# First attention of a Flamingo-style block: the query bias by full-width products, zero writes moved in the load queue, weight splits dealt out otherwise

## The chip, the cores and the metric

The kernel is one program on one core of a Trainium2 chip. The metric is device time in microseconds (us) of one execution; the time quoted is the median of several executions. Engines are named as in the profile: PE (matrix products), PEld (its weight loads), DVE, ACT, POOL (the vector, activation and general engines) and SP, which here only issues transfers. ACTq and SPq are the issuing sequencers of ACT and SP.

## The reference

Eight batches of 256 rows x 256 columns pass through four residual parts: attention over 120 context rows, a mixture of experts with two of twelve experts per row (eight real, four that return the row itself), a second attention with 16 heads, and a product in 8-bit floats. The change touches the first of them and the work that lies beside it:

```python
x = x + jnp.tanh(g_xattn[0]) * _L0_xattn_ref(_layernorm(x, axis=-1), ctx_512, ctx_512, ...)
x = x + jnp.tanh(g_ffn[0]) * _L0_ffn_ref(_layernorm(x, axis=-1), ...)
...
q = jnp.einsum('bld,de->ble', query, Wq) + bq
k = jnp.einsum('bld,de->ble', key, Wk) + bk
v = jnp.einsum('bld,de->ble', value, Wv) + bv
scores = jnp.einsum('bqe,bke->bqk', q, k)
attn = jax.nn.softmax(scores, axis=-1)
out = jnp.einsum('bqk,bke->bqe', attn, v)
```

The query bias `bq` reaches the scores as one number per key, `bq . k`, the same for every query row.

## The kernel before

The program is written engine by engine, each engine with its own hand-written order; semaphores tie them. The first attention and the gate of the experts run as a software pipeline over `t in range(B + 9)`, B = 8 batches, called slots here. A batch b goes through these functions, each in a later slot of its engine:

- DVE `stats0(b)`, POOL `root0(b)`, ACT `norm0(b)` (L649): the first layer norm. PE `transpose_x0(b)` (L1557), ACT `copy_xT(b)`.
- PE `keys0(b)` (L1531), ACT `copy_kt0(b)` (L623), PE `keys_by_query(b)`: the keys are multiplied by the query weights (L1542) and by the query bias (L1545, a stationary operand of one column, result 1 x 120). DVE `copy_kq(b)` (L991) and `copy_bqk(b)` (L995) bring the two results to SBUF. PE `values0(b)` (L1552), DVE `copy_v0(b)`.
- PE `scores0(b)`: first L1571, which puts the bias row under all 128 query rows of two halves (contraction over one partition, 240 columns), then L1577, the scores proper. DVE `max0_of(b)`, ACT `exp0_of(b)` (L636), PE `transpose_prob(b)` (L1586), ACT `copy_probT(b)` (L643), PE `attend(b)` (L1594).
- DVE `add_x1(b)`, `stats1(b)`, POOL `root1(b)` (L497, L499), ACT `norm1(b)` (L658): the second layer norm. SP stores its result in `xn_d` (L439). PE `transpose_x1(b)` (L1557 again), DVE `copy_xT1(b)` (L1026), PE `gate_of(b)` (L1611), DVE `logits_of(b)` (L1036).

`norm1(b)` writes one of two buffers and so waits for the store of batch b - 2 to have landed:

```python
act.wait_ge(rstd1_ok, b + 1)
...
wait(act, xn_stored[b % 2], 16 * (b // 2))
```

Beside this, the expert weights (8.4 MB) come in as eight loads `chunk_in[0..7]` of four chunks each, and each of the 32 chunks is split into a high part, on ACT by `high(j)` (L668), and a low part, on POOL by `low(j)` (L513) or for four chunks on DVE by `low(j)` (L1032). `low(j)` needs `high(j)`, and both take the chunks in rising order. `HIGH_FROM`, `LOW_FROM`, `LOW_LATE`, `VECTOR_LOW` and `VECTOR_FROM` say from which slot on a place in an engine's slot takes a chunk. Also beside it, `clear_y()` on ACT writes zeros (4.2 MB) into the experts' output buffer `y_d` in HBM by five transfers.

After the slots, DVE picks the two experts of every row (the chain from L1056 `top` over L1059 `eq`, L1060 `cand`, L1064 `pick`, L1065 `hot`, L1068 `left`, first for 12 of the 16 row tiles, `EARLY`, then for the last four), ranks the rows and builds the lists by which POOL gathers rows for the experts. The order on every engine is the order of its loop body; nothing reorders it.

Of the kernel before, what the change touches and what calls it, by code (L numbers as in the profile page):

```python
# [90 lines left out]
def build(nc, x, ctxT, wq0T, wk0, wv0, bq0, bk0, bv0, gateT, gbias, wmoe, wq1, wk1, wv1, wo1,  # L91
          bq1, bk1, bv1, bo1, wfT, bf, gains, c_ident, c_tri, c_count, c_token, c_head, out):
    ctx = ExitStack()
    with ctx:
# [52 lines left out]
        kq = sb("kq", [P, B * C * LK], F32, kv)  # L147
        v0 = sb("v0", [LK, B, D + 1], F32, kv)
        bqk = sb("bqk", [1, B * LK], F32, kv)
# [141 lines left out]
        def sems(names):  # L291
# [11 lines left out]
        (kt_done, kt_ok, kq_done, kq_ok, bqk_ok, v0_done, v0_ok) = sems(  # L303
            "kt_done kt_ok kq_done kq_ok bqk_ok v0_done v0_ok")
# [104 lines left out]
        HIGH_FROM, LOW_FROM = (8, 2, 2, 2), (4, 4, 9, 3)  # L409
        EARLY, FAR = TILES - 2 * U, 64 * P  # L410
        AHEAD, ZERO_LOADS = 6, 1 + 2 * TILES * D // ZEROS
        VECTOR_LOW, VECTOR_FROM = (7, 10, 13, 16), 5
        LOW_LATE = {B: 3, B + 1: 4, B + 2: 3, B + 3: 2, B + 4: CHUNKS}

        @block.sync
        def _(sp):
# [10 lines left out]
            for m in range(LOADS):  # L427
                c = cols(m, PER_LOAD * CHUNK)
                sp.dma_start(wl[:, c].bitcast(F32), wmoe[:, c]).then_inc(chunk_in[m], 16)
                if m == 0:  # L430
                    sp.dma_start(x4[:, 4:B, :], xv[:, 4:B, :]).then_inc(x_late_in, 16)
                    for dst, src in late:
                        sp.dma_start(dst, src).then_inc(con_in, 16)
                    sp.dma_start(bv1_sb[:], bv1.rearrange("o (c p) -> p (o c)", p=P),
                                 allow_slow_non_contiguous=True).then_inc(con_in, 16)
# [172 lines left out]
        def _(act):  # L608
# [69 lines left out]
            def clear_y():  # L678

                act.wait_ge(zero_ok, 1)  # L680
                act.dma_start(xn_d[0:1, :], wh[0:1, E_FFN * WE - D:].bitcast(F32)).then_inc(zeroed, 16)
                y_p = y_d[1:1 + 2 * TILES * P, :].rearrange("(p r) n -> p (r n)", p=P)
                for c in range(0, 2 * TILES * D, ZEROS):
                    act.dma_start(y_p[:, c:c + ZEROS], wh[:, E_FFN * WE - ZEROS:].bitcast(F32)).then_inc(zeroed, 16)

            for t in range(B + 9):
                if t == B - 1:
                    clear_y()
# [8 lines left out]
                high_next(t, 2)  # L697
# [267 lines left out]
        def _(dve):  # L965
# [22 lines left out]
            def copy_kq(b):  # L988

                dve.wait_ge(kq_done, b + 1)  # L990
                dve.tensor_copy(kq[:, cols(b, C * LK)], bank[1][:, 0:C * LK]).then_inc(kq_ok, 1)  # L991

            def copy_bqk(b):
                dve.wait_ge(kq_done, b + 1)
                dve.tensor_copy(bqk[0:1, cols(b, LK)], bank[1][0:1, C * LK:(C + 1) * LK]).then_inc(bqk_ok, 1)  # L995
# [529 lines left out]
        def _(pe):  # L1525
# [9 lines left out]
            def keys_by_query(b):  # L1535
# [3 lines left out]
                wait(pe, bqk_ok, b)  # L1539
# [26 lines left out]
            def scores0(b):  # L1566
                pe.wait_ge(xT_copied, b + 1)
                pe.wait_ge(kq_ok, b + 1)
                pe.wait_ge(bqk_ok, b + 1)
                wait(pe, exp_done, b)  # L1570
                pe.matmul(bank[6][:, 0:U * LK], ones[0:1, :],  # L1571
                          bqk[0:1, cols(b, LK)].unsqueeze(1).to_broadcast([1, U, LK]), start=True, stop=False,
                          skip_group_check=True)
                for u in range(U):
                    for c in range(C):
                        k = b * C * LK + c * LK
                        ins = pe.matmul(bank[6][:, u * LK:(u + 1) * LK], xT[:, b % 2, c * S + u * P:c * S + u * P + P],  # L1577
                                        kq[:, k:k + LK], start=False, stop=(u == U - 1 and c == C - 1),
                                        skip_group_check=True)
# [552 lines left out]
```

## Time and profile before

| | us |
|---|---|
| median of 3 runs | 381.73 (381.43 to 382.63) |
| the profiled execution, its own time | 380.27 |
| its span, first to last instruction | 378.5 |
| slots of the first attention, PE from batch 0's transposes to the last logits | 10.7 to 72.6 |

The rows below are from the profiled execution. A row of a timeline gives start, length, engine, line, operation, tiles, shapes and count; a bracket at the end is the engine's idle time before the row and what ended it. Lengths of neighbouring rows on PE overlap, since products are pipelined; the chain that ended last gives lengths without overlap. Time between the last slot and the end (the experts, the second attention, the last product) is not touched.

### The profile page before, as it was taken

Reading aid. Unit: us, or ns where it says so; the run is one execution under the profiler, and the core shown is the slowest. Engines: PE = TensorE matmul, PEld = TensorE weight load, DVE = VectorE, ACT = ScalarE, POOL = GpSimd, SP = SyncE. Lnnn points to the kernel's source line nnn. Section 1 sums busy time; section 2 is a strip of 40 time slices with the busy share of each in tenths; the row PEclk is TensorE's granted clock in tenths of the full one; section 3 lists DMA queues with packets and bytes.
Section 4 is the critical chain, followed back from the end, with each engine's and each line's share of the span. In section 5 each row is a group of like instructions: output and inputs, shape, how many; then the busy total and the mean of one; then the engine's idle time right before and its main releaser. Section 6 shows DMA issues by size and latency. Waiting matters only on the chain.

```text
span 378.5 us, 9200 instructions
## 1 busy us (share of the span) xinstructions
PE 348.6 (92%) x3030; PEld 277.8 (73%) x3031; DVE 260.1 (69%) x669; ACT 219.1 (58%) x455; POOL 159.2 (42%) x215
## 2 busy tenths in 40 slices
PE   1999999976999999999999998879999999999995
PEld 0888787654799999999999993556667666666773
DVE  1569879895655665555445447878888989776785
ACT  1687899612454445445444542466777778665585
POOL 7497599505355655565555435321131132102000
PEclk9999999999999999999999999999999999999999
DMA  6999752301224334323333214310111000000004
GB/s 184 312 413 399 296 241 85 113 2 55 79 75 134 102 102 132 104 78 69 78 75 76 63 58 138 114 58 5 55 58 57 2 2 2 3 3 2 2 33 189
DMA packets 15386, 38.25 MB, mean 101 GB/s; under 512 B 3574, under 2 KB 4748, under 8 KB 13820
## 3 DMA queue, kind: packets, MB, share of 16 engines
q1 hardware_dynamic: 9978, 22.55, 17.1%
q0 software_dynamic: 3936, 10.45, 9.4%
q10 hardware_dynamic: 1442, 4.85, 3.3%
q8 instruction: 19, 0.31, 0.4%
q14 instruction: 11, 0.09, 0.1%
HBM read 24.34 MB, written 13.50 MB: 100 GB/s over the span
## 4 chain that ended last, share of the span: by engine, by line
PE 77%; DVE 9%; ACT 6%; DMA 3%; issue 3%; POOL 1%; ACTq 1%; DVEq 0%; POOLq 0%
PE two L1716 15%; PE two L1729 14%; PE two L1865 5%; PE two L1748 4%; PE two L1895 4%; PE two L1930 4%; PE two L1851 4%; PE two L1831 3%; PE two L1739 2%; PE two L1577 2%; PE two L1542 2%; PE two L1922 2%; PE two L1557 2%; PE two L1911 1%; DMA kmask<-in_c_head 1%
## 5 line engine op out<-in xcount | busy, mean ns | idle before, releaser
L1207 DVE SCALAR_TENSOR_TENSOR gate<-th,two 128x512 f32<-128x512 f32 x39 | 26.8, 688 | 58.3 <-ACT th L739 32.4
L739 ACT ACTIVATE th<-two 128x512 f32<-128x512 f32 x39 | 23.3, 599 | 70.9 <-PE two L1729 43.1
L546 POOL DMA_INDIRECT y_d<-y_sb,goal_i x39 | 38.4, 986 | 50.7 <-ACT y_sb L749 50.7
L540 POOL DMA_INDIRECT xg<-xn_d,slot_i x39 | 37.8, 970 | 31.2 <-DVE slot_i L1160 13.8
L1716 PE MATMUL two<-wh,gh 128*128 x156 | 44.2, 283 | 0.1
L1716 PE MATMUL two<-wh,gl 128*128 x156 | 44.0, 282 | 0.0
L1716 PE MATMUL two<-wl,gh 128*128 x156 | 43.8, 281 | 0.0
L560 POOL TENSOR_TENSOR rstd<-var,half 128x2 f32<-128x2 f32 x14 | 9.8, 700 | 76.9 <-DVE var L1274 76.9
L1307 DVE TENSOR_REDUCE nm<-two 128x8 f32<-128x960 f32 x32 | 36.1, 1152 | 4.5 <-PE two L1851 4.1
L513 POOL TENSOR_TENSOR wl<-wl,wh 128x512 fp32r<-128x512 f32 x28 | 35.3, 1277 | 7.0 <-ACT wh L668 6.9
L1729 PE MATMUL two<-wh,xh 128*128 x78 | 34.2, 438 | 1.3 <-DVE xl L1201 1.3
L837 ACT ACTIVATE pT<-two 120x1024 f32<-120x1024 f32 x32 | 31.1, 1037 | 7.0 <-PE two L1865 7.0
L1716 PEld LDWEIGHTS two<-wh,gh 128*128 128x128 f32 x156 | 29.5, 189 | 3.6 <-issue 0.3
L1716 PEld LDWEIGHTS two<-wl,gh 128*128 128x128 f32 x156 | 29.4, 188 | 3.3
L1716 PEld LDWEIGHTS two<-wh,gl 128*128 128x128 f32 x156 | 29.4, 188 | 3.2
L1729 PE MATMUL two<-wl,xh 128*128 x78 | 30.9, 396 | 0.0
L1729 PE MATMUL two<-wh,xl 128*128 x78 | 30.7, 394 | 0.0
L1211 DVE TENSOR_TENSOR gl<-two,gh 128x512 fp32r<-128x512 f32 x39 | 27.0, 691 | 2.7 <-ACT gh L744 1.1
L744 ACT ACTIVATE gh<-two 128x512 fp32r<-128x512 f32 x39 | 23.6, 605 | 0.1
L1748 PE MATMUL two<-ident,gate 128*128 128x128 f32 x156 | 23.3, 272 | 0.0
L734 ACT ACTIVATE xh<-two 128x256 fp32r<-128x256 f32 x39 | 15.7, 403 | 9.4 <-PE two L1739 9.4
L971 DVE BATCH_NORM_STATS2 stat<-x_sb 128x6 f32<-128x256 f32 x32 | 12.0, 417 | 11.9 <-DMA x_sb<-in_x 11.7
(272 smaller groups left out, 885.0 us busy)
## 6 DMA issues: line engine op xcount, KB each, us to landing
wl<-in_wmoe SPq DMA_DIRECT2D x8, 1024.0 KB, 14.9
y_d<-wh ACTq DMA_DIRECT2D x4, 1024.0 KB
yg<-y_d SPq DMA_DIRECT2D x7, 512.0 KB, 3.6
xn_d<-xq SPq DMA_DIRECT2D x8, 256.0 KB, 2.0
xz<-xn_d SPq DMA_DIRECT2D x8, 256.0 KB
out_x<-of SPq DMA_DIRECT2D x8, 256.0 KB, 2.0
x_sb<-in_x SPq DMA_DIRECT2D x1, 1024.0 KB, 9.9
x_sb<-in_x SPq DMA_DIRECT2D x1, 768.0 KB, 4.6
```

Of the source, the lines that this page charges most:

```text
L513: pool.tensor_tensor(wl[:, c], wl[:, c].bitcast(F32), wh[:, c], ALU.subtract).then_inc(split_l, 1)
L540: pool.indirect_dma_start(xg[:, n % 2, :], None, xn_d, bass.IndirectOffsetOnAxis(ap=slot_i[:, n:n + 1], axis=0)).then_inc(gathered[n % 2], 16)
L546: pool.indirect_dma_start(y_d, bass.IndirectOffsetOnAxis(ap=goal_i[:, n:n + 1], axis=0), y_sb[:, n % 2, :], None).then_inc(y_stored[n % 2] ...
L739: nc.scalar.activation(th[:], bank[2 + k][:], ACT.Tanh, scale=0.5).then_inc(th_ok, 1)
L744: nc.scalar.activation(gh[:, k, :], bank[4 + k][:], ACT.Copy).then_inc(gh_ok, 1)
L837: nc.scalar.activation(pT[:, r, p, :], ring(ring_of_keys(b, r) + p)[0:LK, :], ACT.Exp).then_inc(e_ok, 1)
L1207: dve.scalar_tensor_tensor(gate[:, k, :], th[:], 1.0, bank[2 + k][:], ALU.add, ALU.mult).then_inc(gate_ok, 1)
L1211: dve.tensor_tensor(gl[:, k, :], bank[4 + k][:], gh[:, k, :], ALU.subtract).then_inc(gl_ok, 1)
L1307: dve.tensor_reduce(nm[:, u, 2 * HG * p:2 * HG * (p + 1)].rearrange("p (j h) -> p j h", j=2), src.rearrange("p j (h k) -> p j h k", k=LK), ...
L1716: ins = pe.matmul(bank[6 + k][:, 0:D], (gl if part == 2 else gh)[:, k, a], (wl if part == 1 else wh)[:, bass.ds(e + (C * FF + c * D), D)], ...
L1729: ins = pe.matmul(bank[2 + k][:], (xl if part == 2 else xh)[:, k, c * P:(c + 1) * P], (wl if part == 1 else wh)[:, bass.ds(e + c * FF, FF) ...
L1748: ins = pe.transpose(bank[4 + k][:, c * P:(c + 1) * P], gate[:, k, c * P:(c + 1) * P], ident[:])
```

## The change

Three edits. The bias product L1545 now has a stationary operand of the whole array (the bias column repeated 128 times), so its result is 128 x 120, is copied with the rest of `kq` in one DVE copy, and feeds L1571's successor from all 128 partitions with a stationary operand that repeats the first column of the identity. `clear_y()` leaves ACT; SP issues the same five transfers ahead of the last two weight loads. The tables that deal out the splits are changed, and ACT skips one place in slots 6 and 7.

```diff
-        kq = sb("kq", [P, B * C * LK], F32, kv)
+        kq = sb("kq", [P, B, (C + 1) * LK], F32, kv)
...
-        HIGH_FROM, LOW_FROM = (8, 2, 2, 2), (4, 4, 9, 3)
+        HIGH_FROM, LOW_FROM = (8, 8, 2, 2), (4, 9, 9, 3)
+        BUSY_SLOTS = (6, 7)
...
-        VECTOR_LOW, VECTOR_FROM = (7, 10, 13, 16), 5
-        LOW_LATE = {B: 3, B + 1: 4, B + 2: 3, B + 3: 2, B + 4: CHUNKS}
+        VECTOR_LOW, VECTOR_FROM = (13, 16, 19, 22), 9
+        LOW_LATE = {B: 3, B + 1: 4, B + 2: 3, B + 3: 3, B + 4: CHUNKS}
...
             for m in range(LOADS):
+                if m == LOADS - 2:
+                    sp.wait_ge(zero_ok, 1)
+                    sp.dma_start(xn_d[0:1, :], wh[0:1, E_FFN * WE - D:].bitcast(F32)).then_inc(zeroed, 16)
+                    y_p = y_d[1:1 + 2 * TILES * P, :].rearrange("(p r) n -> p (r n)", p=P)
+                    for c in range(0, 2 * TILES * D, ZEROS):
+                        sp.dma_start(y_p[:, c:c + ZEROS], wh[:, E_FFN * WE - ZEROS:].bitcast(F32)).then_inc(zeroed, 16)
...
-            def clear_y():
...
-                if t == B - 1:
-                    clear_y()
...
-                high_next(t, 2)
+                if t not in BUSY_SLOTS:
+                    high_next(t, 2)
...
-                dve.tensor_copy(kq[:, cols(b, C * LK)], bank[1][:, 0:C * LK]).then_inc(kq_ok, 1)
-
-            def copy_bqk(b):
-                dve.wait_ge(kq_done, b + 1)
-                dve.tensor_copy(bqk[0:1, cols(b, LK)], bank[1][0:1, C * LK:(C + 1) * LK]).then_inc(bqk_ok, 1)
+                dve.tensor_copy(kq[:, b, :], bank[1][:, 0:(C + 1) * LK]).then_inc(kq_ok, 1)
...
-                    ins = pe.matmul(bank[1][0:1, C * LK:(C + 1) * LK], bq0_sb[:, c:c + 1], kt0[:, b % 2, c, :],
-                                    start=(c == 0), stop=(c == C - 1))
+                    ins = pe.matmul(bank[1][:, C * LK:(C + 1) * LK], bq0_sb[:, c:c + 1].to_broadcast([P, P]),
+                                    kt0[:, b % 2, c, :], start=(c == 0), stop=(c == C - 1))
...
-                pe.matmul(bank[6][:, 0:U * LK], ones[0:1, :],
-                          bqk[0:1, cols(b, LK)].unsqueeze(1).to_broadcast([1, U, LK]), start=True, stop=False,
+                pe.matmul(bank[6][:, 0:U * LK], ident[:, 0:1].to_broadcast([P, P]),
+                          kq[:, b, C * LK:(C + 1) * LK].unsqueeze(1).to_broadcast([P, U, LK]), start=True, stop=False,
```

What the tables do, counted from the code: high parts done by the end of slot 7, 18 before and 10 now (in slots 2 to 7 before three a slot; now two a slot in 2 to 5, one in 6 and 7); before two more stood ahead of `norm1(2)` in slot 8 and now too, so 20 before and 12 now. The rest: before 12 from there to slot 11; now 20, up to slot 13, with four between `norm1(5)` and `norm1(6)` and four between `norm1(6)` and `norm1(7)`, where none stood before. Low parts on POOL before slot 8: 13 before, 9 now. DVE's four stood in slots 5 to 8 and stand in slots 9 to 12.

Three places in the orders. First SP's queue. Before, the last loads are followed by the weights of the last product (`wf_sb`) and the eight stores of the second norm:

```order
L434 DMA bv_sb<-in_bv 128x2x1
L429 DMA wl<-in_wmoe 128x2048 x7
L436 DMA wf_sb<-in_wfT 128x512
L439 DMA xn_d<-xq 128x512 x8
L445 DMA wq_sb<-in_wq 128x512
```

Now:

```order
L440 DMA bv_sb<-in_bv 128x2x1
L435 DMA wl<-in_wmoe 128x2048 x5
L430 DMA xn_d<-wh 1x256
L433 DMA y_d<-wh 128x2048 x4
L435 DMA wl<-in_wmoe 128x2048 x2
L442 DMA wf_sb<-in_wfT 128x512
L445 DMA xn_d<-xq 128x512 x8
```

The five zero writes moved into SP's queue, ahead of two loads, `wf_sb` and every store. Second, ACT from `copy_xT(5)` at the end of slot 6 to slot 7 and 8. Before (L681 and L684 are `clear_y`, the L658 is `norm1(1)`):

```order
L630 ACTIVATE xT<-two 128x512
L681 DMA xn_d<-wh 1x256
L684 DMA y_d<-wh 128x2048 x4
L623 ACTIVATE kt<-two,bk_sb 128x120 x2
L668 ACTIVATE wh<-wl 128x512
L636 ACTIVATE prob<-two,negmax 128x120 x2
L658 ACTIVATE xq<-x_sb,less,rstd 128x256 x2
L668 ACTIVATE wh<-wl 128x512
L649 ACTIVATE xq<-x_sb,less,rstd 128x256 x2
L643 ACTIVATE probT<-two 120x256
L668 ACTIVATE wh<-wl 128x512
L630 ACTIVATE xT<-two 128x512
```

Now, from `copy_kt0(7)` on (the first L664 is `norm1(1)`, the second `norm1(2)` of slot 8):

```order
L629 ACTIVATE kt<-two,bk_sb 128x120 x2
L642 ACTIVATE prob<-two,negmax 128x120 x2
L664 ACTIVATE xq<-x_sb,less,rstd 128x256 x2
L655 ACTIVATE xq<-x_sb,less,rstd 128x256 x2
L649 ACTIVATE probT<-two 120x256
L674 ACTIVATE wh<-wl 128x512
L636 ACTIVATE xT<-two 128x512
L674 ACTIVATE wh<-wl 128x512 x2
L642 ACTIVATE prob<-two,negmax 128x120 x2
L664 ACTIVATE xq<-x_sb,less,rstd 128x256 x2
L674 ACTIVATE wh<-wl 128x512
L649 ACTIVATE probT<-two 120x256
```

The transfers and two of three high parts of slot 7 are gone; `norm1(2)` stands ahead of `copy_probT(5)`. Third, POOL's last low parts, from `root1(4)` in slot 9 on. Before:

```order
L497 TENSOR_TENSOR rstd<-var,half 128x2
L499 TENSOR_TENSOR less<-less,rstd 128x2
L513 TENSOR_TENSOR wl<-wl,wh 128x512 x4
L497 TENSOR_TENSOR rstd<-var,half 128x2
L499 TENSOR_TENSOR less<-less,rstd 128x2
L513 TENSOR_TENSOR wl<-wl,wh 128x512 x3
L497 TENSOR_TENSOR rstd<-var,half 128x2
L499 TENSOR_TENSOR less<-less,rstd 128x2
L513 TENSOR_TENSOR wl<-wl,wh 128x512 x2
L497 TENSOR_TENSOR rstd<-var,half 128x2
L499 TENSOR_TENSOR less<-less,rstd 128x2
L513 TENSOR_TENSOR wl<-wl,wh 128x512 x3
```

Now:

```order
L503 TENSOR_TENSOR rstd<-var,half 128x2
L505 TENSOR_TENSOR less<-less,rstd 128x2
L519 TENSOR_TENSOR wl<-wl,wh 128x512 x4
L503 TENSOR_TENSOR rstd<-var,half 128x2
L505 TENSOR_TENSOR less<-less,rstd 128x2
L519 TENSOR_TENSOR wl<-wl,wh 128x512 x3
L503 TENSOR_TENSOR rstd<-var,half 128x2
L505 TENSOR_TENSOR less<-less,rstd 128x2
L519 TENSOR_TENSOR wl<-wl,wh 128x512 x3
L503 TENSOR_TENSOR rstd<-var,half 128x2
L505 TENSOR_TENSOR less<-less,rstd 128x2
L519 TENSOR_TENSOR wl<-wl,wh 128x512 x6
```

One more low part stands ahead of `root1(7)`, the last pair of L503 and L505, and six behind it where there were three.

## Rows read from the trace of the kernel before

**Rows 1.** Busy time of each engine, clock and DMA, two stretches of the slots
```profile
core 0: us, PE busy (x) PEld busy (x) DVE busy (x) ACT busy (x) POOL busy (x), PEclk, DMA share, GB/s
...
42.00:52.50 10.50, 10.20 (x76) 8.47 (x74) 8.25 (x27) 8.45 (x21) 8.83 (x11) 1.00 0.98 398
10.70:61.70 51.00, 50.70 (x337) 41.78 (x336) 39.08 (x145) 41.50 (x99) 38.68 (x48) 1.00 0.78 305
```

**Rows 2.** The chain that ended last, one slot: start, length, what
```profile
32.21 0.44 PE two L1557 x4
32.65 0.89 PE two L1542 x8
33.54 0.50 PE two L1545 x4
34.04 0.36 PE two L1586 x2
...
35.27 0.60 PE two L1571 x2
35.87 1.08 PE two L1577 x8
36.95 0.89 PE two L1594 x4
```

**Rows 3.** Timeline of the weight loads in the same slot
```profile
35.80 0.97 PEld L1577 LDWEIGHTS two<-kq,xT 128*128 128x128 f32 x8 [0.30 <-issue]
```

**Rows 4.** Timeline of ACT and its sequencer at the zero writes
```profile
41.53 2.27 ACTq L684 DMA_DIRECT2D y_d<-wh  x2
43.91 0.61 ACT L623 ACTIVATE kt<-two,bk_sb 128x120 f32<-128x120 f32 x2 [1.87 <-issue]
```

**Rows 5.** Groups of DVE in the slots: busy us, mean ns, idle before
```profile
L991 DVE COPY kq<-two 128x240 f32<-128x240 f32 x8 | 3.2, 401 | 2.4 <-PE two L1545 2.4
L995 DVE COPY bqk<-two 1x120 f32<-1x120 f32 x8 | 2.1, 260 | 0.0
```

**Rows 6.** SP queue rows; issue to landing of bk_sb, L429, L439 (in this order)
```profile
11.20 0.82 SPq L433 DMA_DIRECT2D bk_sb<-in_bk  x1
...
39.30 30.07 SPq L439 DMA_DIRECT2D xn_d<-xq  x8
...
bk_sb<-in_bk SPq DMA_DIRECT2D x1, 1.0 KB, 9.2
...
L429 SPq DMA_DIRECT2D wl<-in_wmoe x8: 432/498/1726, 9.2 to 17.4; - x8
...
DMA to landing us min/median/max: 7.6/14.9/22.0
...
DMA to landing us min/median/max: 2.0/2.0/7.9
```

**Rows 7.** Timeline of ACT from norm1(2) to norm1(7)
```profile
50.69 1.11 ACT L658 ACTIVATE xq<-x_sb,less,rstd 128x256 f32<-128x256 f32 x2
...
61.91 1.66 ACT L668 ACTIVATE wh<-wl 128x512 fp32r<-128x512 f32 x3
63.47 2.18 ACT L658 ACTIVATE xq<-x_sb,less,rstd 128x256 f32<-128x256 f32 x4
67.94 1.09 ACT L658 ACTIVATE xq<-x_sb,less,rstd 128x256 f32<-128x256 f32 x2 [2.29 <-POOL less L499]
```

**Rows 8.** Timeline of POOL, the last slots
```profile
53.49 4.97 POOL L513 TENSOR_TENSOR wl<-wl,wh 128x512 fp32r<-128x512 f32 x4
...
66.94 0.69 POOL L497 TENSOR_TENSOR rstd<-var,half 128x2 f32<-128x2 f32 x1
...
67.86 3.86 POOL L513 TENSOR_TENSOR wl<-wl,wh 128x512 fp32r<-128x512 f32 x3
```

**Rows 9.** Timeline of DVE, the choice of experts
```profile
69.33 1.26 DVE L1060 SCALAR_TENSOR_TENSOR cand<-eq,count 128x144 f32<-128x144 f32 x1
70.62 0.69 DVE L1026 COPY xT<-two 128x512 f32<-128x512 f32 x1
...
71.82 0.31 DVE L1065 TENSOR_TENSOR hot<-cand,pick 128x144 f32<-128x144 f32 x1
72.17 0.31 DVE L1068 SCALAR_TENSOR_TENSOR left<-hot,logit 128x144 f32<-128x144 f32 x1
...
74.06 0.21 DVE L1065 TENSOR_TENSOR hot<-cand,pick 128x48 f32<-128x48 f32 x1
```

More of the change, by code:

```diff
@@ L146, in build @@
         kv = ExitStack()
-        kq = sb("kq", [P, B * C * LK], F32, kv)
+        kq = sb("kq", [P, B, (C + 1) * LK], F32, kv)
         v0 = sb("v0", [LK, B, D + 1], F32, kv)
-        bqk = sb("bqk", [1, B * LK], F32, kv)
         kv.close()
@@ L301, in build @@
         p1_mm, p1_act = sems("p1_mm p1_act")
-        (kt_done, kt_ok, kq_done, kq_ok, bqk_ok, v0_done, v0_ok) = sems(
-            "kt_done kt_ok kq_done kq_ok bqk_ok v0_done v0_ok")
+        (kt_done, kt_ok, kq_done, kq_ok, v0_done, v0_ok) = sems(
+            "kt_done kt_ok kq_done kq_ok v0_done v0_ok")
         (xq_ready, xT_done, xT_copied, scores_done, max_done, exp_done, probT_done, probT_copied, pv_done, x1_done,
@@ L676, in high_next @@
                         high(j)
-            def clear_y():
[L680 to L684, printed above, removed]
             for t in range(B + 9):
-                if t == B - 1:
-                    clear_y()
                 if t < B:
@@ L1072, in _ @@
                     stats0(t)
-                if 0 <= t - 3 < B:
-                    copy_bqk(t - 3)
                 if t == 3:
@@ L1538, in keys_by_query @@
                 wait(pe, kq_ok, b)
-                wait(pe, bqk_ok, b)
                 for m in range(C):
@@ L1568, in scores0 @@
                 pe.wait_ge(kq_ok, b + 1)
-                pe.wait_ge(bqk_ok, b + 1)
                 wait(pe, exp_done, b)
-                pe.matmul(bank[6][:, 0:U * LK], ones[0:1, :],
-                          bqk[0:1, cols(b, LK)].unsqueeze(1).to_broadcast([1, U, LK]), start=True, stop=False,
+                pe.matmul(bank[6][:, 0:U * LK], ident[:, 0:1].to_broadcast([P, P]),
+                          kq[:, b, C * LK:(C + 1) * LK].unsqueeze(1).to_broadcast([P, U, LK]), start=True, stop=False,
                           skip_group_check=True)
@@ L1575, in scores0 @@
                     for c in range(C):
-                        k = b * C * LK + c * LK
                         ins = pe.matmul(bank[6][:, u * LK:(u + 1) * LK], xT[:, b % 2, c * S + u * P:c * S + u * P + P],
-                                        kq[:, k:k + LK], start=False, stop=(u == U - 1 and c == C - 1),
+                                        kq[:, b, cols(c, LK)], start=False, stop=(u == U - 1 and c == C - 1),
                                         skip_group_check=True)
```

## The prediction

> **What bounds the kernel now.** I read the busy table by stretches first. From 10.7 to 61.7 us PE is busy 50.70 of 51.00 us [rows 1], so in the slots the first suspect is PE's own work. The chain that ended last says the same for one slot: pieces of PE without a gap, about 5.6 us a slot [rows 2]. From 62 us on the chain leaves PE. ACT's timeline shows `norm1(7)` at 67.94 us after 2.29 us of waiting for POOL's L499 [rows 7], and POOL's shows why: `root1(7)` starts at 66.94 behind low parts [rows 8]. Behind it stand one pass through PE, the copy at 70.62 and the choice of experts on DVE [rows 9]. So the stage ends on a chain ACT, POOL, DVE, and PE's time counts only as far as it lets these begin earlier. What matters is therefore when `norm1(7)` can run, and what DVE meets after it.
>
> **Part 1, the bias products.** In the slot shown, eight passes of L1542 (120 columns) take 0.89, 0.111 each; the four of L1545 take 0.50, 0.125 each; the two of L1586 right behind (128 columns) take 0.36, while four passes of L1557 of the same width take 0.44, 0.110 each [rows 2]. L1571 takes 0.60 for two passes of 240 columns; 257 columns cost 0.89 / 4 = 0.22 a pass in L1594, so 0.41 would be expected. L1577 takes 1.08 for eight passes like L1542's, and its weight loads stood idle for 0.30 us before the first one [rows 2, 3]. The excess stands at both edges of the two products that use one column or one row of the array. With full-width operands I price the slot at 0.05 (L1545) + 0.14 (L1586) + 0.19 (L1571) + 0.19 (L1577) = 0.57 us less. Bounds: nothing, if the excess has another cause, and 0.57. Over eight batches that is 4.6 us of PE. The Trainium skill, TensorEngine Tiling (Array Packing), Key Properties, has that a change of tiling mode drains the array; the excess at the edges is in line with it.
>
> On DVE the copy of the bias row goes (0.26 each) and `kq`'s grows from 240 to 360 columns, at most half of 0.40 more [rows 5]: between 0.26 saved and nothing a slot, hidden in DVE's own idle time (10.5 us stretch: busy 8.25 [rows 1]). I count 0. If that cover were gone it would be at most 8 x 0.26 = 2 us, as a gain.
>
> **Part 2, the zeros.** On ACT the issue of the writes goes: it held `copy_kt0(7)` back by 1.87 us [rows 4]. PE had work then, so this is worth nothing alone.
>
> On SP's queue the zeros cost. A transfer of 1 KB issued at 11.20 landed 9.2 us later, behind the megabytes ahead of it in that queue, and the last weight load, issued at 17.4, landed 22.0 us later, at 39.4 [rows 6]. The queue serves in order. The zeros are 4.19 MB, and while zeros were written the rate was 398 GB/s [rows 1], so they put 10.5 us ahead of the last two loads: these land by 49.9. For the weights that is harmless, since chunk 24 is wanted in slot 11. But behind them, in the same queue, stand `wf_sb` and the stores of the second norm. The store of batch 0, issued at 39.30 before and landing in 2.0 [rows 6], now waits: 0.26 MB of `wf_sb` and 0.26 MB of its own add 1.3 us, so it lands at about 51.2 us, no matter how early it is issued. `norm1(2)` waits for it.
>
> Without that wait `norm1(2)` would start at about 46.5: 50.69 [rows 7] less what PE saves up to slot 8 (some six and a half slots of 0.57 = 3.7) and about half a microsecond of ACT's. So ACT idles for some 4.5 us, and everything queued on it behind (`copy_probT(5)`, `copy_xT(7)`, all later high parts) with it; `attend(5)` on PE waits for the first, POOL's low parts for the last. `norm1(2)` starts 0.5 us later than before: the whole gain of parts 1 and 2 up to there is gone.
>
> A rule speaks for the change here. The Trainium skill, DMA: Bandwidth & Descriptors, Issuing engines are not separate DMA queues, says that the queues of all engines run on the same 16 DMA engines and that spreading saves only the issue time. By it the move from ACT's queue to SP's would be free for the store; that is rival C below. The 1 KB row says that order within a queue is kept, and I take the row.
>
> **Part 3, the splits.** Before, from the start of `norm1(2)` at 50.69 to the end of `norm1(7)` at 69.03 ACT took 18.3 us with 12 high parts, 2.3 of it the wait for POOL [rows 7]. Now 20 high parts lie there. One takes 0.52 us of ACT's pace (three from 61.91 to 63.47 [rows 7]), so eight more are 4.2. ACT alone: 51.2 + 18.3 - 2.3 + 4.2 = 71.4; if its other waits of about 1 us vanish too, 70.4.
>
> POOL: by the stall it has done 12 low parts, and the 13th needs the high part behind `norm1(2)`, ready at 52.7. One low part takes 4.97 / 4 = 1.24 [rows 8]. The eighteenth high part comes at about 57.8 by the ACT order; from there to `root1(7)` stand seven low parts (8.7), two roots (0.9 each by the step from 66.94 to 67.86 [rows 8], 1.8) and two turns of about 0.55 that DVE's own low parts take from POOL. That is 68.9, and `root1(7)` ends at 69.8. So `norm1(7)` runs until 70.8 by POOL and 70.4 to 71.4 by ACT; I take 71.2, against 69.03: +2.2.
>
> Then six low parts are left for POOL where three were, 69.8 + 6 x 1.25 = 77.3, and DVE has to work beside them. What that costs stands in one row: `cand` of 144 elements took 1.26 us [rows 9] while POOL ran its three low parts from 67.86 [rows 8], where `hot` and `left` of the same width took 0.31 each after POOL was done [rows 9]. That is 0.95 of waiting: until the low part in progress ended. Four instructions of this kind (two operands in SBUF) meet low parts between the copy for batch 7 and the last `hot`: `hot` and `left` of the first 12 tiles, `eq` and `cand` of the last four. Each waits between 0 and 1.25 us, and each makes POOL wait for it a little, so POOL ends at about 78. The copy now starts at about 71.9 (0.44 for PE's transposes, as L1557 [rows 2], and the hand-overs); from there DVE would without waiting reach the last `hot` in 3.4 us (70.62 to 74.06 [rows 9]), at 75.3. With the waits it gets there when POOL is through with `eq` or `cand`: 78.5. Against 74.06 that is +4.5. From there on nothing is changed and I pass it on in full. The skill's SBUF — State Buffer, Who interferes with whom, states this lock for a DVE instruction with two SBUF inputs against a GpSimd instruction that reads SBUF, held for the whole instruction; the 1.26 us row agrees.
>
> DVE's four low parts cost ACT and PE nothing before; now the one of slot 9 needs the fourteenth high part (53.5) and holds `copy_v0(7)` behind it, for which `transpose_x1(2)` waits; that is PE idle time inside the stall, covered by ACT's 20 us behind it.
>
> **Sum.** -4.6 (PE) is not on the path; store wait, eight high parts, POOL's order: +2.2; low parts beside the choice of experts: +2.3; together +4.5. The profiled execution took 380.27, so 384.8 on its scale. The median of the runs is 381.73, 1.5 above it; on that scale 386.2.
>
> **The rivals** (times on the median's scale). A change of 0.3%, 1.1 us, is about what a measurement of this kernel can tell from none.
>
> A, as above: 384.5 to 388.0. For it: two independent floors, ACT's and POOL's, give the same time. Against it: it needs the store's wait.
>
> B, the store waits, but POOL does not hold DVE. For it: the trace has a single wait of this kind, that of `cand`, and it may have had another cause. Against it: its length fits the low part beside it. Then +1.3 to +2.4 (2.2, less up to 0.95 that the one `cand` lost before): 383.0 to 384.1.
>
> C, faster: the store does not wait for the zeros, because the DMA engines take it between them. Then `norm1(2)` starts at 46.5, ACT's 20 us fit the earlier end of PE's slots, and `norm1(7)` ends near 66.5: -2.5, with `root1(7)` near 65.4 and low parts until 73. If these hold DVE up as in A, only -0.5 is left. 379.2 to 381.2. For it: a store issued while ACT's queue wrote zeros took 7.9 us at most [rows 6]. Against it: the 1 KB row. It decides where the store of batch 0 lands: before 48 us C, after 50 A or B.
>
> D, worse: PE sits idle for about 5 us between the last products for the second attention and the ranking, and comes back at the lower clock, which these rows don't show in the slots; its work of 5 us before the slot lists would then be late as well: +6 to +8, 387.8 to 389.8.
>
> That the bias products don't get faster changes A little, since PE isn't on its path.
>
> **How the numbers follow.** A 0.50, B 0.17 (0.03 of it within 0.3%), C 0.24 (0.18 faster, 0.06 within), D 0.09. Faster 0.18, within 0.3% 0.09, slower 0.73. The time is A's, 386.2. The range 379.8 to 388.4 leaves out about half of C's faster part and most of D; A's own is 384.5 to 388.0.
>
> **What would show it.** Right: L1571 and L1577 together near 1.3 us a slot instead of 1.68; ACT idle 4 to 5 us before the L664 of batch 2, released by a transfer at 51 us; `norm1(7)` ending near 71; the last low part of POOL at 77 to 78; `hot`, `left`, `eq` or `cand` of about 1.2 us where 0.2 to 0.3 stood. Wrong: an L664 of batch 2 before 49 us; a weight load or store landing out of order; low parts over by 73 us.

## The result and the profile after

The changed kernel takes 389.75 us (median of 4 runs, 388.25 to 390.89), the kernel before 382.18 beside it (381.43 to 383.01): ratio 1.0205, 95% interval 1.0175 to 1.0236. It is 7.6 us slower. The direction was forecast; the time lies 1.4 us above the upper end of the range and 3.6 above the forecast. The profiled execution took 390.76 us (span 389.0). Two runs that took over 1.5% longer than the fastest of their kernel are left out of the ratios: one of the kernel before in the last batch (845.88 us) and one of `bias_splits` (388.64 us; without it its median of 385.45 would be 385.25).

The chain that ended last, in one slot of the changed kernel (start, length, what, as in [rows 2]):

```profile
31.25 0.44 PE two L1547 x4
...
32.57 0.45 PE two L1535 x4
33.02 0.22 PE two L1574 x2
...
34.10 0.41 PE two L1560 x2
34.52 0.88 PE two L1565 x8
...
36.28 0.44 PE two L1547 x4
```

From one L1547 to the next it is 5.03 us where it was about 5.6 [rows 2]: the two bias products and their neighbours got cheaper by what was forecast, 0.57 us a slot (L1535 0.45 instead of 0.50, L1574 0.22 instead of 0.36, L1560 0.41 instead of 0.60, L1565 0.88 instead of 1.08).

The stores of the second norm on SP's queue (one line's instructions: count, issue time, landing), and ACT's timeline around `norm1(2)`, L664:

```profile
L445 SPq DMA_DIRECT2D xn_d<-xq x8: 319/320/326, 37.7 to 73.7; - x8
...
DMA to landing us min/median/max: 2.0/2.0/12.5
```
```profile
46.09 0.61 ACT L642 ACTIVATE prob<-two,negmax 128x120 f32<-128x120 f32 x2
50.28 1.09 ACT L664 ACTIVATE xq<-x_sb,less,rstd 128x256 f32<-128x256 f32 x2 [3.58 <-POOL less L505]
...
58.30 0.38 ACT L649 ACTIVATE probT<-two 120x256 f32<-120x256 f32 x1 [1.67 <-PE two L1574]
...
72.58 1.09 ACT L664 ACTIVATE xq<-x_sb,less,rstd 128x256 f32<-128x256 f32 x2 [0.65 <-POOL less L505]
```

The first store, issued at 37.7, lands 12.5 us later, at 50.2, where it took 2.0 before [rows 6]. ACT stands idle for 3.58 us and starts at 50.28, 0.9 before the forecast 51.2. The bracket names POOL's L505 of another batch (it is that of `root1(4)`, counted by the low parts between the roots), which ended at 50.25; in other kernels of this study the same wait is put down to `DMA xn_d<-xq`. `norm1(7)`, the last row, starts at 72.58 where it started at 67.94 [rows 7]: 4.6 us later, where 2.2 were forecast.

DVE and PE, after that wait:

```profile
52.71 1.07 DVE L1025 TENSOR_TENSOR wl<-wl,wh 128x512 fp32r<-128x512 f32 x1 [2.76 <-ACT wh L674]
53.70 0.47 DVE L993 SCALAR_TENSOR_TENSOR v<-two,gain,bv0g 120x256 f32<-120x256 f32 x1
```
```profile
54.32 0.63 PE L1547 MATMUL two<-ident,xq 128*128 128x128 f32 x4 [3.01 <-DVE v L993]
54.78 1.46 PE L1582 MATMUL two<-v,probT 120*128 120x257 f32 x4
56.03 1.75 PE L1599 MATMUL two<-gate_sb,xT 128*128 128x32 f32 x8
```

`norm1(2)` ended at 51.37, and PE went on only at 54.32, behind `copy_v0(7)` (L993), which stood behind DVE's low part of slot 9 (L1025) as the prediction had said. L1599 takes 1.75 us here for what takes 0.98 at full clock. The stretches say why (the columns are those of [rows 1]; the third figure from the right is the granted clock):

```profile
50.00:54.00 4.00, 1.31 (x11) 1.10 (x9) 1.29 (x2) 3.72 (x8) 1.71 (x3) 1.00 0.18 68
54.00:58.00 4.00, 3.68 (x18) 3.47 (x19) 2.40 (x8) 2.30 (x6) 2.26 (x2) 0.66 0.17 66
58.00:62.00 4.00, 4.00 (x18) 3.78 (x17) 2.50 (x10) 2.70 (x7) 2.64 (x4) 0.50 0.00 0
70.00:74.00 4.00, 2.80 (x14) 2.12 (x15) 2.92 (x8) 3.35 (x8) 3.92 (x5) 0.79 0.17 66
74.00:78.00 4.00, 3.63 (x19) 2.64 (x17) 2.59 (x5) 2.49 (x7) 4.00 (x4) 0.78 0.41 139
86.00:90.00 4.00, 4.00 (x12) 3.10 (x12) 3.69 (x11) 1.60 (x5) 0.00 (x0) 0.58 0.02 4
98.00:102.00 4.00, 3.33 (x11) 2.46 (x10) 1.39 (x6) 0.77 (x2) 1.90 (x2) 0.50 0.15 46
```

The kernel before has 1.00 in all of these in its profiled execution. In the changed one the clock falls to 0.50, that is 1.2 of 2.4 GHz, four times up to 103 us, each time soon after PE stood idle. Taken in steps of 1 us it is low for some 6.8 us from 55.3 (PE idle 3.01 us ahead of 54.32), 3.4 us from 72.3 (idle 1.12 and 1.59 us ahead of 67.37 and 71.20), 3.4 us from 86.0 (3.35 us ahead of the ranking) and 6.8 us from 96.2 (2.04 us ahead of the first blocks of the experts). The last two idle times:

```profile
84.64 0.23 PE L1664 MATMUL two<-pairs,tri 128*128 128x136 bf16 x1 [3.35 <-DVE pairs L1111]
...
96.39 1.65 PE L1653 MATMUL two<-wh 128*128 128x512 f32 x3 [2.04 <-issue]
...
99.55 0.79 PE L1717 MATMUL two<-wh,xh 128*128 x1 [0.67 <-DVE xl L1192]
```

The idle time of 2.04 us is there before as well, with the same length (2.03 us), but in the profiled execution the clock stayed up behind it.

POOL and DVE at the choice of experts, in that order:

```profile
71.59 0.68 POOL L503 TENSOR_TENSOR rstd<-var,half 128x2 f32<-128x2 f32 x1
...
72.50 7.60 POOL L519 TENSOR_TENSOR wl<-wl,wh 128x512 fp32r<-128x512 f32 x6
```
```profile
73.97 1.26 DVE L1053 SCALAR_TENSOR_TENSOR cand<-eq,count 128x144 f32<-128x144 f32 x1
...
77.73 1.25 DVE L1058 TENSOR_TENSOR hot<-cand,pick 128x144 f32<-128x144 f32 x1
79.01 1.26 DVE L1061 SCALAR_TENSOR_TENSOR left<-hot,logit 128x144 f32<-128x144 f32 x1
...
81.92 0.21 DVE L1058 TENSOR_TENSOR hot<-cand,pick 128x48 f32<-128x48 f32 x1
```

POOL has six low parts behind its last root where it had three [rows 8], and `hot` and `left` take 1.25 instead of 0.31 [rows 9]. The last `hot` comes at 81.92 against 74.06: +7.9 where +4.5 was forecast. From there to the first product of the experts another 1.2 is lost (99.55 against 90.44), up to the sixth 1.3 more at half the clock; behind that nothing. The span is 10.5 us longer than that of the profiled execution before.

### The profile page after: what moved, and what is told of

The parts are those of the page before. It is cut to its first block, busy times and chain, and to the rows that moved or that the text cites. A ratio compares the mean times of both kernels' runs of the same rounds, so it can differ in the third digit from the quotient of the medians.

```text
span 389.0 us, 9185 instructions
## 1 busy us (share of the span) xinstructions
PE 351.8 (90%) x3030; PEld 286.5 (74%) x3031; DVE 263.4 (68%) x661; ACT 219.3 (56%) x455; POOL 160.4 (41%) x215
## 4 chain that ended last, share of the span: by engine, by line
PE 76%; DVE 8%; ACT 5%; DMA 5%; issue 3%; POOL 1%; SPq 1%; ACTq 0%; DVEq 0%
PE two L1717 15%; PE two L1704 14%; PE two L1853 5%; PE two L1736 4%; PE two L1883 4%; PE two L1918 4%; PE two L1839 3%; PE two L1819 3%; DMA x_sb<-in_x 3%; PE two L1727 2%; PE two L1582 2%; PE two L1565 2%; PE two L1910 2%; PE two L1547 1%; PE two L1899 1%
## 5 line engine op out<-in xcount | busy, mean ns | idle before, releaser
L519 POOL TENSOR_TENSOR wl<-wl,wh 128x512 fp32r<-128x512 f32 x28 | 36.2, 1309 | 11.1 <-ACT wh L674 11.1
```

Of the source, the lines that this page charges most:

```text
L519: pool.tensor_tensor(wl[:, c], wl[:, c].bitcast(F32), wh[:, c], ALU.subtract).then_inc(split_l, 1)
```

## The experiments

Each kernel ran 6 to 12 times beside the kernel before; ratios are to it. "Clock" is the mean granted clock over a run.

**The three parts, alone and together.**

> The kernel before with the query bias by products of the whole array alone: the zeros stay on ACT, the split tables stay old. Theory (PE's saving of 0.57 us for each slot lies beside ACT's and DVE's work, which sets the slots' length): 381.3 to 382.8, no change. Rival (PE sets the slots' length, 8 slots by 0.57 less what DVE's wider copy costs): 378 to 380.5. Other rival (PE's shorter passes let its clock fall in the longer idle times): 384 or more.

> The kernel before with the zeros on SP's queue alone. Theory (the store of batch 0 lands at about 50, where norm1(2) of the kernel before starts at 50.7 anyway): norm1(2) at 50 to 51, no wait of over 0.5 us on it, 381.5 to 382.8, the same as before. With the bias the slots are 1.6 us earlier there and the wait shows (bias_zeros 381.4 against 379.8). Rival 1 (the queue order costs 1.6 here too): 383.3 to 384.5. Rival 2 (the zeros leave ACT's queue and free ACT): 380 to 381.

> The kernel before with the new split tables alone (no high part on ACT in the third place of slots 2 to 7 and of the busy slots, DVE's and POOL's low parts later, six of POOL's low parts last). Theory (eight high parts more after slot 7 and POOL's six low parts beside DVE's `hot` and `left`): 385.5 to 388, as much over before as the kernel with bias and splits is over that with the bias alone (5.7). Rival 1 (the new tables are made for the shorter slots and are worse without them by more): 388 or more. Rival 2 (the tables cost only through PE's clock, which does not fall here because PE is busier): 382.5 to 384.5.

> Query bias by products of the whole array and zeros on SP's queue, with the split tables of the kernel before. It stands to the kernel with the bias alone (379.8, 2.6 below before) as the zeros' move alone. Theory (the store of batch 0 lands behind the zeros at about 50 and holds norm1(2), whatever the tables are): norm1(2) starts at 50 to 50.5, and 382.5 to 385.5. Rival 1 (the zeros cost only together with the new tables, since ACT has slack without them): 379.5 to 381. Rival 2 (PE's idle time brings its clock down as in the changed kernel): 386 to 388.

> The changed kernel with the zeros back on ACT, behind slot 6's work as before; query bias and split tables stay changed. Theory: as with the stores on ACT, since the zeros are gone from ahead of the store: 384.5 to 386.5, the rest over 382.2 being the splits' order (six low parts of POOL beside DVE's `hot` and `left`, which take 1.2 us each instead of 0.31). Rival 1 (the zeros' move is neutral): 388 to 391. Rival 2 (the zeros' move is all of the loss): 381.5 to 383.

> The changed kernel with the query bias of the kernel before. Theory (with the zeros ahead of the store of batch 0, norm1(2) can't start before 50, so what the bias saves in slots 3 to 8 is lost in that wait): 388.5 to 391, the same as the changed kernel (389.8). Rival (the bias saves 2.6 here too): 391.5 to 393.5.

The zeros' edit, as it is undone in `bias_only`, `splits_only` and `bias_splits`; the other two parts are undone by their own lines of the diff ahead of the prediction:

```diff
-                if m == LOADS - 2:
-                    sp.wait_ge(zero_ok, 1)
...
+                if t == B - 1:
+                    clear_y()
```

```
bias zeros splits   median us   ratio    95% interval       clock, mean
 x                   379.76     0.9929   0.9904 to 0.9954   0.993
       x             381.43     0.9978   0.9958 to 0.9999   0.992
            x        389.85     1.0192   1.0156 to 1.0228   0.981
 x     x             381.40     0.9977   0.9949 to 1.0005   0.989
 x          x        385.45     1.0072   1.0046 to 1.0098   0.981
       x    x        388.50     1.0183   1.0147 to 1.0220   0.986
 x     x    x        389.75     1.0205   1.0175 to 1.0236   0.970
```

The bias alone is a gain of 0.7%, which I had expected for none; the rival "378 to 380.5" has it. In its profile `norm1(2)` starts at 49.12 instead of 50.69 [rows 7]. With the splits alone the bias is worth more, 1.2% (1.0192 without it, 1.0072 with it). With the zeros on SP it is worth nothing: 0.9978 without it, 0.9977 with it, and with the splits there too 1.0183 and 1.0205. The zeros cost only where the bias gains: 0.5% on top of the bias (the two intervals just touch), 1.3% on top of bias and splits, nothing on top of the kernel before or of the splits alone. The timelines of ACT show the exchange. Zeros alone first, bias and zeros behind:

```profile
48.54 0.61 ACT L642 ACTIVATE prob<-two,negmax 128x120 f32<-128x120 f32 x2
50.42 1.09 ACT L664 ACTIVATE xq<-x_sb,less,rstd 128x256 f32<-128x256 f32 x2 [1.26 <-DMA xn_d<-xq]
```
```profile
47.11 0.63 ACT L642 ACTIVATE prob<-two,negmax 128x120 f32<-128x120 f32 x2
49.88 1.09 ACT L664 ACTIVATE xq<-x_sb,less,rstd 128x256 f32<-128x256 f32 x2 [2.13 <-DMA xn_d<-xq]
```

The work ahead ends 1.4 us earlier, the wait is 0.9 longer, and `norm1(2)` starts only 0.5 earlier: the landing of the store sets the start. Most of the loss is the splits': 1.4 to 2.3% in every pair that differs by them.

Three more expectations missed. `splits_only` came out in its first rival's range (388 or more), not at 385.5 to 388. `bias_zeros` (381.4) lies below the theory's 382.5 to 385.5 and above the first rival's 379.5 to 381. `zeros_only` has the time within 0.1 us, but its wait is 1.26 us, not under 0.5.

**The store of batch 0.**

> The changed kernel, with the stores of batches 0 and 1 issued by ACT on its own queue behind norm1 and norm0 of the slot, so that the zeros on SP's queue are no longer ahead of them. Theory (norm1(2) is held by the store of batch 0, which lands 12.5 us after its issue instead of 2.0; the 3.0 us in which PE then stands idle bring its clock down for 6 us; the splits and POOL's low parts beside DVE's choice of experts cost the rest): norm1(2) starts by 47.5 instead of 50.28, no idle time of PE over 1.5 us before 66, granted clock 1.00 from 54 to 62, and 384.5 to 386.5 us. Rival 1 (the store is not the cause, norm1(2) is late because of POOL's root or the order of ACT's work): norm1(2) still near 50 and 388 to 391. Rival 2 (the store is all of it): 381.5 to 383.

```diff
+                if 0 <= t - 6 < 2:
+                    store(t - 6)
...
-            for b in range(B):
+            for b in range(2, B):
                 sp.wait_ge(xq1_ready, b + 1)
```

386.20 us, 1.0095 (1.0062 to 1.0129); zeros and splits are as in the changed kernel, and the two stores land after at most 8.2 us. `norm1(2)` starts at 45.91 instead of 50.28 (the prediction had 46.5 without the wait). That gives back about half of the 1.0205, and the kernel ends beside `bias_splits` (1.0072). `store(b)` is the old transfer, issued by ACT behind norm0(t). So the zeros cost by that store, as forecast. But the clock did not stay up. It fell later (stretches of this kernel):

```profile
50.00:54.00 4.00, 2.75 (x22) 2.49 (x22) 3.29 (x6) 3.29 (x8) 3.56 (x3) 1.00 0.02 8
66.00:70.00 4.00, 2.49 (x14) 1.58 (x14) 1.96 (x7) 2.76 (x7) 3.92 (x5) 0.78 0.17 66
70.00:74.00 4.00, 3.91 (x14) 2.98 (x14) 0.69 (x1) 2.85 (x9) 4.00 (x5) 0.50 0.33 118
```

My expectation of 1.00 up to 62 held, that of a clock loss confined to the stall did not: from 68.2 to 81.9 the clock was low, behind idle times of 0.59 and 1.28 us.

**PE kept busy.**

> The changed kernel with products of no use on PE where it stands idle: six 256-column ones ahead of the transposes of batch 2 (idle 3.01 us), two and three ahead of those of batches 5 and 6, seven 512-column ones ahead of the wait for `pairs`, and five more ahead of the wait for the block table. No wait is taken away. Theory (about 5.8 us of the loss are PE's work at half the clock after its idle times: 3.4 up to the choice of experts, 2.4 from there to the first blocks of the experts): granted clock 1.00 from 54 to 110, the first h product block takes 1.7 us instead of 2.9, 383.5 to 386.5 us. Rival (the clock falls in times when PE is not on the path, and the loss is the waits alone): 388.5 to 391.

> The changed kernel with products of no use in the two late idle times of PE alone (seven ahead of the wait for `pairs`, five ahead of the wait for the block table), none in the slots. Theory (the low clock after the ranking and in the first blocks of the experts costs some 2.5 of the loss, that of slots 9 and 10 the rest): mean clock 0.975 to 0.985, 386.5 to 388.0. Rival 1 (the slots' low clock is what matters): 388.5 to 390. Rival 2 (the late low clock is all): 384 to 386.

> Bias and new split tables, zeros on ACT (385.4 at a mean clock of 0.981 before), with the same products of no use in the two late idle times. Theory (single runs of one kernel lie 3 to 4 us apart between clock 0.98 and 1.00, and bias and splits ran at 0.981 where bias alone had 0.993): clock 0.993 or more, 382.0 to 383.8; what is then left over bias_late (378.2) is the waits, about 4. Rival (clock and time only go together because a late chain leaves PE idle, and the time does not fall with the idle time filled): 385 to 386.

> The kernel before with the query bias by products of the whole array, and with seven products of no use ahead of the wait for `pairs` and five more ahead of the wait for the block table. In the kernel with the bias alone the granted clock was 0.82 and 0.75 in 86 to 94. Theory (this is PE's clock after its idle time of 2.07 us, and it costs the first blocks of the experts 1 to 1.5 us): clock 1.00 there, 378.0 to 379.3. Rival (the first blocks wait for the gathers, not for PE): 379.4 to 380.2.

```diff
 in the slots (warm and warm_hold), ahead of transpose_x1
+                if t in {9: 6, 12: 2, 13: 3}:
+                    pe.wait_ge(logit_kept, t - 8)
+                    filler({9: 6, 12: 2, 13: 3}[t])
 behind them (all four)
+            busy(bank[5], 7)
             pe.wait_ge(pairs_ok, 1)
...
-            busy(bank[5], 5)
+            busy(bank[5], 10)
             pe.wait_ge(blocks_kept, 1)
```

`warm`: 387.59 (1.0157, 1.0124 to 1.0191), clock 0.992 instead of 0.970. No wait was taken away, and the time falls by about 2 us, less than I had expected (383.5 to 386.5), though the products hold PE up somewhat themselves (two of their three places in the slots began late, behind their own wait). In its profile every stretch up to 110 us has clock 1.00. `norm1(7)` starts at 70.75, `pairs` at 81.38, the first product of the experts at 95.40:

```profile
49.79 1.09 ACT L664 ACTIVATE xq<-x_sb,less,rstd 128x256 f32<-128x256 f32 x2 [3.83 <-DMA xn_d<-xq]
...
70.75 1.09 ACT L664 ACTIVATE xq<-x_sb,less,rstd 128x256 f32<-128x256 f32 x2 [1.10 <-POOL less L505]
```

With the clock out of the way the changed kernel is late by +2.8 at `norm1(7)` (67.94 before) and by +5.0 at `pairs` (76.43 before) and at the experts (90.44 before). The forecast had +2.2 and +4.5. `after_late`, without products in the slots: 388.86 (1.0173, 1.0142 to 1.0204), clock 0.980; that is above the 386.5 to 388.0 of my theory, inside the rival's 388.5 to 390. The interval overlaps those of both neighbours, so how much of it is won in the slots and how much behind is not settled. `splits_warm`: 383.68 (1.0044, 1.0018 to 1.0070) instead of 385.45, clock 0.989 where I had expected 0.993 or more. `bias_late`: 378.16 (0.9898, 0.9870 to 0.9926), clock 0.998, the fastest kernel of the study, 1.0% below the kernel before. Its time is as expected; the clock of 1.00 behind the added products is not quite, since its profile has 0.61 in 82 to 86 us.

How sure is this? In every pair with and without the added products (`warm` and `after_late` against the changed kernel, `splits_warm` against `bias_splits`, `bias_late` against `bias_only`, and `pool_warm` against `pool_late` below) the two intervals overlap. But all five ratios fall, by 0.0028 to 0.0048, and the clock rises in all five. That more work on PE shortens the time is shown by the five together, not by any one of them.

The runs without any edit go the same way. The kernel before ran 90 times in four batches: its nine runs at clock 0.999 took 379.8 to 380.4 us, its twelve at 0.982 took 383.6 to 384.3. It is one program, and the two groups are 3.8 us apart. By itself this shows only that clock and time go together; which drives the other is what the added products show. The execution whose profile I had read was one at 0.999.

**POOL's low parts beside DVE.**

> The changed kernel with the products of no use on PE as before, and with POOL's last six low parts held back until DVE has made `pairs`. PE's clock stays at full level in both, so the difference to the kernel with the products alone (387.6) is the low parts beside DVE's choice of experts. Theory (each operand pass of DVE beside them takes 1.2 us instead of 0.31): `eq`, `cand` and `left` of 12 tiles take 0.31 each instead of 1.14 to 1.27, `pairs` comes 1.5 to 2.9 us earlier, and 384.7 to 386.3. Rival 1 (DVE's passes are long for another reason): `pairs` unmoved and 387 to 388. Rival 2 (the held low parts are late for the experts): PE waits for the low parts ahead of the experts, 388 or more.

```diff
                 root1(t - 5)
+                if t == B + 4:
+                    pool.wait_ge(pairs_ok, 1)
                 for j in itertools.islice(pieces, LOW_LATE[t]):
                     low(j)
```

391.60 (1.0250, 1.0217 to 1.0283), worse than `warm`: rival 2's time, but not for its reason. Before the experts PE waited not for the low parts but for DVE's `onerow` (4.32 us idle ahead of 90.28), and the clock did not stay up as I had assumed (0.50 in 90 to 94, mean 0.987). Where the low parts are gone, DVE is quick, and where they now are, it is slow:

```profile
72.19 0.31 DVE L1054 TENSOR_TENSOR eq<-logit,top 128x144 f32<-128x144 f32 x1
72.53 0.31 DVE L1055 SCALAR_TENSOR_TENSOR cand<-eq,count 128x144 f32<-128x144 f32 x1
...
75.34 0.31 DVE L1063 SCALAR_TENSOR_TENSOR left<-hot,logit 128x144 f32<-128x144 f32 x1
...
79.98 0.29 DVE L1113 TENSOR_TENSOR pairs<-hot 128x128 bf16<-128x128 f32 x1
...
80.64 1.04 DVE L1118 TENSOR_SCALAR prod<-valid 128x32 f32<-128x32 f32 x1
```

In `warm` these `eq`, `cand` and `left` took 1.14, 1.27 and 1.25 (`hot` between them took 0.31, so not every pass beside a low part waits). `pairs` comes 1.4 us earlier (79.98 against 81.38), but `slot_i` 3.6 later (93.54 against 89.95): the six low parts (80.35 to 87.99) now stand beside the ranking. `prod`, the last row, had taken 0.20 before. The cost goes where the low parts go.

**The tables of the splits one by one**, each on the kernel with the bias alone.

> The kernel with the bias alone (379.8), and of the new split tables only DVE's part: its four low parts (13, 16, 19, 22) stand in slots 9 to 12 instead of (7, 10, 13, 16) in slots 5 to 8. Theory of the splits after the runs so far (they cost 5.7 over the bias alone; DVE's low parts of slots 9 to 12 stand ahead of the next slot's `v` and `negmax` and last 1.0 to 1.5 us each beside POOL's, and that is most of it): 382 to 384. Rival 1 (they replace idle time of DVE in those slots): 379 to 380.8. Rival 2 (they are all of it): 385 or more.

> The kernel with the bias alone, and of the new tables only POOL's: no second low part ahead of root0 in slots 4 to 7, and three low parts instead of two in slot 11, so that more of them fall behind the last roots. Theory (POOL's late low parts reach into DVE's choice of experts, whose passes of two operands then take 1.2 us instead of 0.31): POOL's last low part ends after 72 instead of before 70, one to three of DVE's `hot`, `left` passes at 1.2, 380.5 to 382.5. Rival (POOL's lows start as early since they wait for ACT's high parts anyway): 379 to 380.3.

> The kernel with the bias alone, and DVE's and POOL's new tables together, ACT's high parts in the old order. What is left to the kernel with bias and all splits (385.4) is ACT's table. Theory (the high parts held back in slots 6, 7 and ahead of slot 8 lengthen slots 8 to 10, since ACT then has up to five a slot): 382.5 to 384.5, so ACT's part is 1 to 3. Rival 1 (ACT's table is nothing, low parts are all): 385 to 386. Rival 2 (ACT's table is all): 379 to 381.

> Bias and POOL's part of the new tables (383.4 at a mean clock of 0.988), with the same products of no use. Theory (POOL's three low parts ahead of root1(7) and six beside DVE's choice of experts cost 3.4 us up to `pairs`, of which some is made good behind it, and the clock about 1): clock 0.995 or more, 381.0 to 382.5, 3 to 4 over bias_late. Rival (POOL's part costs by PE's idle time and its clock alone): 378.5 to 380.

```diff
 vector_late                       pool_late (pool_warm: and the products of bias_late)
-VECTOR_LOW, VECTOR_FROM = (7, 10, 13, 16), 5     -LOW_FROM = (4, 4, 9, 3)
+VECTOR_LOW, VECTOR_FROM = (13, 16, 19, 22), 9    +LOW_FROM = (4, 9, 9, 3)
                                                  -LOW_LATE = {..., B + 3: 2, ...}
                                                  +LOW_LATE = {..., B + 3: 3, ...}
```

```
DVE's  POOL's  ACT's   median us   ratio    95% interval       clock, mean
 -      -       -       379.76     0.9929   0.9904 to 0.9954   0.993
 x      -       -       381.42     0.9996   0.9971 to 1.0021   0.989
 -      x       -       383.41     1.0027   0.9995 to 1.0059   0.988
 x      x       -       385.64     1.0101   1.0061 to 1.0141   0.981
 x      x       x       385.45     1.0072   1.0046 to 1.0098   0.981
 -      x       -       381.64     0.9991   0.9970 to 1.0013   0.995   (pool_warm)
```

POOL's table costs 1.0% and DVE's 0.7%, and they add up. ACT's, the one that I had priced, adds nothing: the two rows that have both others, 1.0101 without it and 1.0072 with it, have overlapping intervals, as the rival of `vector_pool` had it (385 to 386). These kernels have the zeros on ACT; that ACT's table costs nothing behind the stall of the changed kernel as well is not tested. Two expectations missed: `vector_late` (381.42) lies below the theory's 382 to 384, and `pool_late` (383.41) above its 380.5 to 382.5. `pool_warm` against `bias_late` (0.9898) is POOL's table with PE busy in both: 0.9%, 3.5 us. Its POOL and DVE, beside those of `bias_late` behind:

```profile
63.10 3.73 POOL L513 TENSOR_TENSOR wl<-wl,wh 128x512 fp32r<-128x512 f32 x3
...
67.76 7.59 POOL L513 TENSOR_TENSOR wl<-wl,wh 128x512 fp32r<-128x512 f32 x6
```
```profile
71.72 1.21 DVE L1062 TENSOR_TENSOR hot<-cand,pick 128x144 f32<-128x144 f32 x1
72.96 1.26 DVE L1065 SCALAR_TENSOR_TENSOR left<-hot,logit 128x144 f32<-128x144 f32 x1
...
78.31 0.29 DVE L1115 TENSOR_TENSOR pairs<-hot 128x128 bf16<-128x128 f32 x1
```
```profile
62.16 2.50 POOL L513 TENSOR_TENSOR wl<-wl,wh 128x512 fp32r<-128x512 f32 x2
...
65.53 3.86 POOL L513 TENSOR_TENSOR wl<-wl,wh 128x512 fp32r<-128x512 f32 x3
```
```profile
69.50 0.31 DVE L1062 TENSOR_TENSOR hot<-cand,pick 128x144 f32<-128x144 f32 x1
69.84 0.31 DVE L1065 SCALAR_TENSOR_TENSOR left<-hot,logit 128x144 f32<-128x144 f32 x1
...
74.47 0.29 DVE L1115 TENSOR_TENSOR pairs<-hot 128x128 bf16<-128x128 f32 x1
```

Three low parts instead of two stand ahead of `root1(7)`, and `norm1(7)` starts at 67.84 instead of 65.62 (+2.2); six instead of three stand beside the choice of experts, and `pairs` is late by 3.84, so 1.6 more. POOL's two numbers alone make the 2.2 us at `norm1(7)` that I had derived from ACT's eight high parts and POOL together, and 1.6 of the 2.3 behind it. What DVE's table costs I can't place: in the profiles of `vector_late` and `bias_only` `pairs` is only 0.25 apart (74.97 and 74.72) and the first product of the experts 0.26. Part of it may be the clock: in the profile of `vector_pool`, `norm1(7)` is 0.24 later than in that of `pool_late` and `pairs` 1.46 later (79.61 and 78.15), with PE's clock at 0.50 from 70 to 78 where `pool_late` has 0.98 to 1.00.

## Why the prediction was right in direction and wrong in size

**Part 1, bias products.** The price of 0.57 us a slot held. "-4.6 (PE) is not on the path" is true of the changed kernel, where the store's wait takes it all (1.0205 with the bias, 1.0183 without; with the old splits 0.9977 and 0.9978). By itself it is on the path: -2.6 us by the medians, `norm1(2)` 1.6 earlier; with the splits and the zeros on ACT it is worth 4.4 us (`splits_only` against `bias_splits`).

**Part 2, the zeros.** Right: queue order, the landing at 50.2 (51.2 forecast), the idle ACT (3.6 us; 4 to 5 forecast), the loss of PE's gain. `norm1(2)` started 0.4 us earlier than before, not 0.5 later. Rival C fell at its own mark: 50.2 is not before 48. The Trainium skill, DMA: Bandwidth & Descriptors, Issuing engines are not separate DMA queues, says that issuing from several engines saves only the issue time. That does not hold for a small store behind megabytes on the same queue: it took 12.5 us here against at most 8.2 from ACT's queue, and the measurement decides.

**Part 3, the splits.** `norm1(7)` +2.2 and the choice of experts +2.3 were +2.8 and +2.1 with the clock held up. The wait of DVE for POOL is shown: the same instructions take 0.31 us without low parts beside them and 1.14 to 1.27 with them. The Trainium skill, SBUF — State Buffer, Who interferes with whom, says that a DVE instruction with two SBUF inputs contends with a GpSimd instruction that reads SBUF (GpSimd is POOL); the trace agrees. Rival B falls. The step "eight more high parts are 4.2" on ACT is not borne out: ACT's table adds nothing to the other two while the zeros are on ACT, in the changed kernel it was ACT that waited for POOL ahead of `norm1(7)` (0.65 us), and POOL's and DVE's tables carry the loss. POOL's own sum is right only if the two turns of DVE's low parts cost 0.55 us together; at 0.55 each it gives 69.4 for the start of `root1(7)`, not 68.9. It came at 69.76 in `warm` and at 71.59 in the changed kernel.

**The step that failed** is the term for PE's idle time, which the sum put at nothing: it held PE's work at the durations of the profiled execution, all at clock 1.00. The idle time inside the stall I called "covered by ACT's 20 us behind it". It was not covered, because behind it PE worked for some 6.8 us at half the clock, and ACT then waited for PE (1.67 us at 58.30). Of the 4.6 us by which `norm1(7)` is late in the profile, 2.8 are left in `warm`, where the clock stayed up (0.5 of the difference stand at `norm1(2)` already). In `store_act`, without the idle time of 3.01 us, PE had clock 1.00 from 54 to 62. The changed kernel ran at a mean clock of 0.970, the one before at 0.990; 3.8 us for 0.017 in the kernel before makes 0.020 worth 4.5 us, and the lines through the runs of the other kernels are mostly flatter (some 150 us for 1.0 over all of them, so 3). The median difference of 7.6 is then some 3 to 4.5 of clock and 3 to 4.5 of waits, for which the sum had 4.5. The split is an estimate: no run of the changed kernel has a high clock, and `warm`, which has, won only 2.2 us and pays for its own products. Rival D had the mechanism, and the time is at the upper end of its range (387.8 to 389.8), but I gave it 0.09 and put it at one place, ahead of the ranking, where the trace then showed four. That its time fits is partly luck, since the place that it named is one of the two short ones.

A second, smaller fault: I took the difference of 1.5 us between the profiled execution and the median as a constant to be added. It goes with the clock as well: that execution had 0.999, the mean is 0.990.

## What to carry to other kernels

A stall on the engine that is busiest can cost more than its length: soon after idle times of 1.1 to 3.4 us PE ran at half the clock for 3.4 to 6.8 us here, though not after every such idle time. Price that in each new idle time, and try a few products of no use in the old ones (7 and 5 here: 0.9929 became 0.9898 with the bias products, the same way as in the other pairs but within the intervals). Before a bulk transfer moves to another queue, list the small transfers queued behind it and who waits for the buffer. When low-priority work of POOL moves later, look at what DVE does with two operands in SBUF at that time.

## What the runs showed that I had not expected

The clock differs from run to run of one program, and the time goes with it: 0.999 and 380.2 us, 0.982 and 384.0 us. The kernels with more idle time on PE have the lower clock (0.970 with idle times of 3.01, 3.35 and 2.04 us, 0.998 with none over 1.2 us up to the experts' start in `bias_late`). The longest idle time is no sure sign, though: even in the profile of `bias_late` the clock was 0.61 in 82 to 86 us. A single profiled execution can hide all this: the idle time of 2.03 us was followed by 1.00 in the profile of before and by 0.82 and 0.75 in two stretches of `bias_only` (2.07 us). Where the clock is lost, it also moves: without the stall at 50 us the lower clock came at 68 to 82 us instead (`store_act`).
